# Post-norm transformer layer on eight cores: transposes moved from TensorE to the SP queue, and a different start

## The reference

```python
Q, K, V = x @ Wq + bq, x @ Wk + bk, x @ Wv + bv      # 16 heads of 64
w = softmax(causal(Q @ K.T / 8))                     # per sequence and head
x = layernorm(x + (w @ V) @ Wo + bo)                 # Wo 1024 x 1024
gate, up = x @ wg.T, x @ wu.T                        # int32 weights / 127, hidden 3072
x = layernorm(x + (silu(gate) * up) @ wd.T)
```

## Time and the profile before

| | |
|---|---|
| median of 3 runs | 1165.81 us (1165.63 to 1166.45) |
| profiled execution, device time | 1166.87 us |
| its span on the slowest core (2) | 1165.2 us |
| spans of the eight cores | 1160.5 to 1165.2 us |
| TensorE busy on core 2 | 1118.3 us, 96% of the span |
| ScalarE, VectorE, Pool busy | 602.1, 390.9 and 87.9 us |
| chain that ended last | PE 93%, issue 2%, DMA 2%, DVE 2%, ACT 1% |

### The profile page before, as it was taken

One profiled execution on the slowest core, in us unless ns is written; L12 is line 12 of the kernel. 1 busy time (PEld: TensorE's weight loads), 2 busy tenths in 40 slices (PEclk: granted clock), 3 DMA queues, 4 the chain that ended last, 5 costly groups with the idle time before them and its releaser, 6 DMA issues.

```text
span 1165.2 us, 28546 instructions; the slowest of 8 cores (1160.5 to 1165.2 us)
## 1 busy us (share of the span) xinstructions
PE 1118.3 (96%) x11460; PEld 676.3 (58%) x11568; DVE 390.9 (34%) x833; ACT 602.1 (52%) x723; POOL 87.9 (8%) x156
## 2 busy tenths in 40 slices
PE   3899999999999999999999999999999999999997
PEld 1676677767676677765555566666444444444443
DVE  0333323333333433335667522222333212121333
ACT  0588889999999899898855411112000111111000
POOL 3000000000000000013010211111000111110000
PEclk9999999999999999999999999999999999999999
DMA  9902100021001103069655764334111345441011
GB/s 128 155 3 38 21 2 3 2 39 21 2 3 21 20 3 74 33 153 244 138 129 109 147 107 73 63 65 73 37 55 55 74 75 82 78 73 19 37 45 66
DMA packets 32200, 74.61 MB, mean 64 GB/s; under 512 B 3648, under 2 KB 9792, under 8 KB 31168
## 3 DMA queue, kind: packets, MB, share of 16 engines
q0 software_dynamic: 26448, 54.80, 28.4%
q1 hardware_dynamic: 5616, 17.91, 4.1%
HBM read 109.65 MB, written 8.91 MB: 102 GB/s over the span
## 4 chain that ended last, share of the span: by engine, by line
PE 93%; issue 2%; DMA 2%; DVE 2%; ACT 1%; POOL 0%; POOLq 0%; DVEq 0%; ACTq 0%
PE ps_s L850 15%; PE ps_s L856 15%; PE bank_o L826 11%; PE ps_s L794 11%; PE ps_s L767 10%; PE ps_u L697 7%; PE ps_u L716 7%; PE ps_u L708 5%; PE ps_u L767 5%; PE ps_u L732 4%; DMA x<-x 2%; PE ps_s L732 1%; PE bank_o L746 1%; ACT PT L897 1%; PE ps_s L753 0%
## 5 line engine op out<-in xcount | busy, mean ns | idle before, releaser
L897 ACT ACTIVATE PT<-ps_s 128x1024 bf16<-128x1024 f32 x510 | 490.2, 1024 | 56.0 <-PE ps_s L794 48.9
L911 ACT ACTIVATE gs<-ps_s 128x384 bf16<-128x384 f32 (+1 forms) x120 | 63.9, 533 | 260.3 <-PE ps_s L850 260.1
L850 PE MATMUL ps_s<-x1T,wgb 128*128 128x384 bf16 (+1 forms) x953 | 195.5, 347 | 0.4
L856 PE MATMUL ps_s<-x1T,wub 128*128 128x384 bf16 (+1 forms) x952 | 195.3, 347 | 0.4
L826 PEld LDWEIGHTS bank_o<-V,PT 128*128 128x128 bf16 x4080 | 155.8, 97 | 46.9 <-issue 23.1
L826 PE MATMUL bank_o<-V,PT 128*128 128x65 bf16 x4080 | 176.4, 193 | 2.4 <-DVE PT L1006 2.0
L794 PE MATMUL ps_s<-Q2T,K2T 64*128 64x256 bf16 (+1 forms) x2736 | 158.4, 244 | 4.0 <-ACT PT L897 1.5
L1028 DVE TENSOR_TENSOR hT<-ps_s,gs 128x384 bf16<-128x384 f32 (+1 forms) x120 | 73.3, 611 | 264.3 <-PE ps_s L856 252.7
L850 PEld LDWEIGHTS ps_s<-x1T,wgb 128*128 128x128 bf16 x960 | 93.8, 98 | 83.2
L856 PEld LDWEIGHTS ps_s<-x1T,wub 128*128 128x128 bf16 x960 | 93.9, 98 | 82.6
L767 PE MATMUL ps_s<-wd_sb,hT 128*128 128x512 bf16 x541 | 120.2, 379 | 0.6
(11 more groups left out here) (57 smaller groups left out, 599.2 us busy)
## 6 DMA issues: line engine op xcount, KB each, us to landing
wgb<-wg POOLq DMA_DIRECT2D x48, 256.0 KB, 4.1
wub<-wu POOLq DMA_DIRECT2D x48, 256.0 KB, 5.1
xq_sb<-bo SPq DMA_DIRECT2D x17, 512.0 KB, 5.2
xq_sb<-xq POOLq DMA_DIRECT2D x17, 512.0 KB, 11.1
y<-y SPq DMA_DIRECT2D x17, 512.0 KB, 2.7
wd_sb<-wd POOLq DMA_DIRECT2D x6, 1024.0 KB, 14.2
x<-x POOLq DMA_DIRECT2D x4, 1024.0 KB, 28.2
wk_sb<-wk POOLq DMA_DIRECT2D x8, 256.0 KB, 4.6
```

The costliest lines, as they stand in the source:

```text
L850: inst = pe.matmul(ps_s[w % 2][:, 0, 0:n], wgb[:, i % 4, ec, :], x1T[:, ec, q:q + n], start=(ec == 0), stop=(ec == NEC - 1))
L856: inst = pe.matmul(ps_s[w % 2][:, 1, 0:n], wub[:, i % 4, ec, :], x1T[:, ec, q:q + n], start=(ec == 0), stop=(ec == NEC - 1))
L897: act.activation(PT[:, no % NSLOT], ps_s[no % 3][:], AF.Exp, scale=SCALE).then_inc(sem_exp, 1)
L911: act.activation(gs[:, no % 2, 0:n], ps_s[no % 2][:, 0, 0:n], AF.Silu, scale=1.0 / 127.0).then_inc(sem_silu, 1)
```

## The change

- The transposes of `o_nat` and of `x1` leave TensorE. SP issues a transposing transfer for each 128x128 block: one or two per block of attention (`rows_in`) and eight per set (`rows_on`), straight into `o_allT` and `x1T`. SP follows VectorE's list, so the loads of bo stand between them in that order. The units T, the transposes behind a block and VectorE's copies are gone.
- The waits move with them. The first wave of a part waits for all the sets of its part (`sem_xt`), a W unit for the transfers of its block (`sem_ot`), and a divide for those of the block two before.
- bv is added when V is copied out of PSUM (an addition in place of a copy), from a tile that holds bv for all 128 partitions (512 KB in place of 4 KB), loaded behind the constants. bo for sets 2 and 3 is loaded at the start.
- The W units may start six steps behind the end of their own block, before five behind the end of the next one.
- TensorE makes 16 products of zeros at the start, three between pieces of x block 0 and six ahead of the first V. Each has 512 columns.
- wk of pair 1 is asked for right behind wv. K(1,0) is done behind V of block 0 in both roles. In role 1 Q(0,0) and Q(0,1) follow it, and K(1,i) goes with block i.

```diff
+            return [('K', 0, 0), ('V', 0, 0), ('V', 0, 1), ('K', 1, 0), ('K', 0, 1), ('Q', 0, 0), ('V', 0, 2),
+                    ('V', 0, 3)]
...
             out += [('K', 0, i), ('V', 0, 2 * i), ('V', 0, 2 * i + 1)]
+            if i == 0:
+                out += [('K', 1, 0), ('Q', 0, 0), ('Q', 0, 1)]
+            else:
+                out += [('K', 1, i)]
             if i == 1:
-                out += [('Q', 0, 0), ('Q', 0, 1)]
...
-        block = self.block_end.index(h)
-        if block:
-            self.pe.append(('O', block - 1))
-        return block
+        return self.block_end.index(h)
...
-            first = self.block_end[nb * (NPAIR - 1) + qt // 2 + 1] // (4 * STEP) + 5
+            first = self.block_end[nb * (NPAIR - 1) + qt // 2] // (4 * STEP) + 6
             rows += [(first, self.steps, ('W', qt, 0)), (first, self.steps, ('W', qt, 1))]
-            if qt:
-                rows.append((first, self.steps, ('T', qt - 1)))
...
+            def rows_in(b):
+                sp.wait_ge(sem_o, b + 1)
+                p, q, n = block_rows(b)
+                for i in range(n // 128):
+                    sp.dma_start(o_allT[:, p, q + 128 * i:q + 128 * i + 128], o_nat[:, b % 2, i, :],
+                                 transpose=True).then_inc(sem_ot[b % 2], 16)
+            def rows_on(qt):
+                sp.wait_ge(sem_n, qt + 1)
+                g = next(i for i, sets in enumerate(plan.groups) if qt in sets)
+                for ec in range(NEC):
+                    sp.dma_start(x1T[:, ec, qt * 128:(qt + 1) * 128], x1[:, qt, ec * 128:(ec + 1) * 128],
+                                 transpose=True).then_inc(sem_xt[g], 16)
...
+            load_bo(2)
+            load_bo(3)
+            for what, no in plan.dve:
+                if what == 'D':
+                    rows_in(no)
+                elif what == 'N' and no < role.nset:
+                    rows_on(no)
...
+            def busy(n):
+                for _ in range(n):
+                    pe.matmul(ps_s[0][:, 0, :], PT[:, 0, 0, 0:128], PT[:, 0, 0, :], start=True, stop=True)
...
                         if a == 0 and i == 0 and ec % 2 == 0:
+                            if ec:
+                                busy(3)
                             pe.wait_ge(sem_x0[ec // 2], 16)
...
                     if first == 0 and unit in plan.first_of:
+                        if a == 0:
+                            busy(6)
                         pe.wait_ge(sem_wv[a % 2], 16 * (a // 2 + 1))
...
-                if hc == 0 and plan.done('T', (q + n - 1) // 128) > seen_ev:
-                    seen_ev = plan.done('T', (q + n - 1) // 128)
-                    pe.wait_ge(sem_ev, seen_ev)
+                if hc == 0:
+                    g = next(k for k, sets in enumerate(plan.groups) if (q + n - 1) // 128 in sets)
+                    pe.wait_ge(sem_xt[g], 16 * NEC * len(plan.groups[g]))
...
-                if b:
-                    rows_in(b - 1)
+                if b >= 2:
+                    dve.wait_ge(sem_ot[b % 2], ot_count(b - 2))
...
             for name, dst in consts:
                 sp.dma_start(dst[:], d[name]).then_inc(sem_const, 16)
+            sp.dma_start(bv_sb[:], d['bv']).then_inc(sem_bv, 16)
...
             pool.dma_start(wv_sb[:, 0], d['wv'][0]).then_inc(sem_wv[0], 16)
+            pool.dma_start(wk_sb[:, 1], d['wk'][1]).then_inc(sem_wk[1], 16)
             pool.dma_start(wq_sb[:, 0], d['wq'][0]).then_inc(sem_wq[0], 16)
...
+            pe.wait_ge(sem_zero, 1)
+            for _ in range(16):
+                pe.matmul(ps_s[0][:, 0, :], PT[:, 0, 0, 0:128], PT[:, 0, 0, :], start=True, stop=True)
```

More of the change, by code:

```diff
@@ L108, in __init__ @@
         self.tiles = [range(h, min(h + 4, n)) for h in range(0, n, 4)]
+        ends = sorted({t[-1] for t in self.tiles} | set(self.block_end))
+        self.pv_count = {h: i + 1 for i, h in enumerate(ends)}
         self.steps = -(-len(self.tiles) // STEP)
@@ L148, in __init__ @@
             self.pass_end.append(len(self.waves) - 1)
+            for q in parts:
+                have = sum(map(len, self.groups))
+                self.groups.append(range(have, -(-(q + part) // 128)))
             q0 = q1
@@ L367, in _network @@
     def _network(self):
-        role, nb = self.role, len(self.block_end)
+        role = self.role
         ring = itertools.cycle((0, 2, 1))
@@ L487, in build @@
     sem_pv = sem('sem_pv')
-    sem_block = sem('sem_block')
+    sem_bv = sem('sem_bv')
     sem_rec = sem('sem_rec')
     sem_o = sem('sem_o')
-    sem_tr = sem('sem_tr')
-    sem_ot = sem('sem_ot')
+    sem_ot = [sem(f'sem_ot{i}') for i in range(2)]
     sem_bn = sem('sem_bn')
@@ L497, in build @@
     sem_n = sem('sem_n')
+    sem_xt = [sem(f'sem_xt{i}') for i in range(5)]
     sem_g = sem('sem_g')
@@ L579, in block_rows, with ot_count, load_bo @@
             return b // nblock, *role.blocks[b % nblock][:2]
+        def ot_count(b):
+            return 16 * sum(block_rows(i)[2] // 128 for i in range(b % 2, b + 1, 2))
         def sync_program(sp):
-            for qt in range(role.nset):
-                if qt < 2:
-                    sp.wait_ge(sem_unit, plan.all_done('V', 3))
-                elif qt == 5:
-                    sp.wait_ge(sem_unit, plan.all_done('K', 7))
-                    sp.wait_ge(sem_unit, plan.all_done('Q', 7))
-                elif qt >= 12:
-                    sp.wait_ge(sem_ev, plan.done('W', xq_slot(qt), 1))
-                sp.dma_start(xq_sb[xq_slot(qt)][:], d['bo']).then_inc(sem_bo[xq_slot(qt)], 16)
+            def rows_in(b):
[10 more added lines that the diff above has]
+                                 transpose=True).then_inc(sem_xt[g], 16)
+            def load_bo(qt):
+                sp.dma_start(xq_sb[xq_slot(qt)][:], d['bo']).then_inc(sem_bo[xq_slot(qt)], 16)
+            load_bo(2)
[5 more added lines that the diff above has]
+                    rows_on(no)
+                elif what == 'E' and no + 1 == plan.all_done('V', 3):
+                    sp.wait_ge(sem_ev, no + 1)
+                    for qt in (0, 1, 4):
+                        load_bo(qt)
+                elif what == 'E' and no + 1 == max(plan.all_done('K', 7), plan.all_done('Q', 7)):
+                    sp.wait_ge(sem_ev, no + 1)
+                    for qt in range(5, 12):
+                        load_bo(qt)
+                elif what == 'E' and plan.units[no] in [('W', xq_slot(qt), 1) for qt in range(12, role.nset)]:
+                    sp.wait_ge(sem_ev, no + 1)
+                    load_bo(plan.units[no][1] + 8)
@@ L649, in gpsimd_program @@
                 load_qk(p)
-            pool.wait_ge(sem_pv, plan.block_end[nblock * 6 - 1] // 4 + 1)
+            pool.wait_ge(sem_pv, plan.pv_count[plan.block_end[nblock * 6 - 1]])
             pool.dma_start(wo_sb[:], d['wo']).then_inc(sem_wo, 16)
-            for qt in range(5):
+            for qt in (2, 3, 0, 1, 4):
                 add_rows(qt)
@@ L664, in load_wd @@
                 pool.dma_start(wd_sb[:, 4 * c:4 * c + 4], d['wd'][:, 4 * c:4 * c + 4]).then_inc(sem_wd, 16)
[L667 removed]
+            pool.wait_ge(sem_pv, len(plan.pv_count))
             for c in range(3):
                 load_wd(c)
[L671 removed]
             load_gu(4)
+            for i in range(2):
+                pool.wait_ge(sem_ot[i], ot_count(len(plan.block_end) - 1 - (len(plan.block_end) - 1 - i) % 2))
             for c in range(3, 6):
@@ L884, in tensor_program @@
                     products(no)
-                elif what == 'O':
-                    block_out(no)
                 else:
```

102 lines of the change are left out of this document (29 added, 73 removed).

## The result

The changed kernel takes 1222.02 us (median; 1220.8 to 1223.49) beside 1165.81 us: a ratio of 1.048 with an interval of 1.046 to 1.050, 56 us slower where 13 us faster was forecast, and outside the range.

What follows compares the result with a forecast made beforehand. TensorE was taken to bound nearly everything. On core 2, 1165.2 - 15.0 - 1.6 + 3.7 = 1152.3 us; the slowest span falls 12.9 us, so 1165.8 becomes 1153 us. The range of 8 in 10 was 1149 to 1172 us.

Steps and rivals of the forecast that it cites:

- What leaves TensorE: Attention-output and row-set transposes, 55 ns each: role 0 saves 15.0 us, role 1 13.2 us, plus 1.6 us on core 2.
- The start: Wait for x block 1: lands 5.4 us later; after work moved in, role 0 loses 3.7 us, role 1 1.9 us.
- Zero products and V's addition: Start and V's copy out of PSUM: neither gains; copy 694 ns, addition 692 ns, zeros' saved time spent waiting.
- the transfers on SP: Transposes on SP's queue at about 0.8 us each: hidden throughout attention and the last pair, so costing nothing.
- I take t at about 0.8 us: Queue time per transpose on SP, between the mask transfer's 0.43 us issue and 2.0 us landing.
- 71 t - 80.2: Wait in us of role 1's wave 4 for 71 transposes at t us each; none up to t = 1.13 us.
- 81 t - 101.1: Core 2's wave 8: 81 transposes at t us each against 101.1 us of room; hidden up to t = 1.25 us.
- the rival (0.30): SP's queue sets the output rows' pace: wave 4 of role 1 waits once t exceeds 1.13 us; chance 0.30.
- In attention a block needs two in 5 to 15 us: always: Attention: SP's transposes for a block are always hidden, at any t considered.
- leave more room or about as much: First waves, a block's divide and five late bo loads: no tighter for SP's transposes than the last pair's waves.
- the rival's 1178 us: SP's queue pacing the output rows: at t = 1.5 us, 26 us of wait at wave 4; rival's chance 0.30.
- By it the prediction had no change: With 1309 ns of queue time per transpose, role 1 waits 12.7 us; whole about 1165 us, no measurable change.

Runs made afterwards that it cites:

- late_held: Kernel before with wk_alone's start and second-pass row sets transposed by SP's transfers, held until wave 24's up products are done: 1161.65 us (0.996).
- wk_alone: Kernel before with only wk of pair 1 early and K(1,0), plus role 1's two Q units, in the wait for x: 1165.51 us (0.9995).
- mix_held: late_held plus attention output of pairs 0 to 6 by SP's transfers with four buffers, V's bias added at its copy from early 128 KB: 1162.58 us (0.9975).
- start_only: The change without any transposing transfer; its start's loads, K order, zero products and V's addition stay: 1170.56 us (1.004).
- loads_alone: Kernel before with only bv whole, two loads of bo ahead of x's block 1, and V's addition: 1170.68 us (1.004).
- late_sets: Kernel before with only the second-pass row sets transposed by SP's transfers, asked for as they are normalised: 1171.13 us (1.004).
- light: The change with wd's loads each one more gate/up tile later and only 128 of 1024 columns of xq and bo loaded: 1204.1 us (1.032).
- the two halves: The change with only attention output by transfers, 1186.64 us (1.017), and with only row sets by transfers, 1199.35 us (1.028).
- bo_pool: The whole change with bo asked for on Pool's queue in place of SP's: 1210.71 us (1.038).

## Why the prediction was wrong, point by point

*What leaves TensorE: right for the row sets, half right for the blocks.* Core 2 has 272 fewer products. The 64 transposes of row sets that late_held moves bring 3.9 us beside wk_alone, where 3.5 were counted. The block transposes bring less. Between the 101st and the 3001st product with V the change gains 5.3 to 5.6 us over the kernel before on the cores of role 0, but wk_alone, which moves K(1,0) and no transpose, gains 2.9 to 3.0. So the 95 block transposes between bring 2.4 to 2.6 us of the 5.2 counted, and mix_held has half of its count too. Why is open.

*The start: right in cause, a little short.* Block 1 was forecast at 33.2 us and came at 34.51 (34.55 on core 3, 34.1 forecast). The forecast of +3.7 us for role 0 stands beside 3.8 us of the whole in start_only and 4.5 in loads_alone (which has none of wk's load and of K(1,0), so 3.8 by the forecast's terms), and wk's load against K(1,0) comes to nothing, as counted.

*Zero products and V's addition: right.* V's copy took 694 ns, the addition takes 693. The zeros ended before what they precede, the clock behind the wait was 0.76 and 0.56 in two stretches of 2.5 us, as in the earlier trace rows, and nothing was gained.

*The step that failed: the transfers on SP.* Three sentences of it were wrong. The first is "I take t at about 0.8 us": an issue takes 1.20 us at the median of core 3 and never less than 1.08, and where it counted, over the 71 up to wave 4 of role 1, it is 1.57 us from one to the next, outside what hides it. The text's own 71 t - 80.2 gives 31 us at 1.57, and 26.3 us were measured. On core 2, the slowest, the 81 up to wave 8 come 1.52 us apart; 81 t - 101.1 gives 22 of the 28.1 us, and the last landing, 16.16 us where 2.0 were counted, is the rest by size. So the mechanism of the rival (0.30) was at work, and the size that was taken for t came from the wrong row. The mask's transfer shares size and shape, but it is 128 rows and no transpose.

The second is "In attention a block needs two in 5 to 15 us: always": it counted SP's time and not the landing. A landing of 2 to 3 us is hidden by two buffers. One of 14 to 28 us isn't, as core 2 has them beside the loads of wo and xq and then of bo, xq and the first gate and up tiles. The third says that the first waves and the divide "leave more room or about as much". The divide cost 19.8 us of TensorE on core 2 and 15.3 on core 3, and the first wave 9.7 us on core 3. Both were named and priced at nothing in every case. On core 3 they are 25 of the 35 us by which it passed even the rival's 1178 us.

*What was missing besides*: that a transpose delays the loads beside it (late_sets; the two waits for wub, 4.5 us together on core 2), and that a slow clock follows each stall. On core 2 that is 6.9 us up to the first wave, by the three stretches above, and 1.6 us behind the stall of 28 us.

*The pages.* The Trainium skill, "VectorE: DVE Perf Modes", The three transpose paths, has 1309 ns for one such transpose through the DMA engines; the trace's 1.2 us of the queue's own time is near it. By it the prediction had no change; the stretch beside the loads, the landings and the slow clock came on top. The Trainium skill, "Advanced Engine Details and Errata", X-Bar Transpose (TRN2), has transposes as fast as other transfers: the trace disagrees, 131 against 375 GB/s, and the measurement decides.

*Open*: the tail of 2 to 3 us in role 0, what stretches the issues in light, why the block transposes bring only half of what was counted, and the 7 us between the two halves (48.7 us with one start) and the whole (56); that both kinds stand in one queue would fit and was not separated.

## What to carry to other kernels

A transfer that replaces work of an engine has three prices: the time of its queue, its landing beside the largest loads that ever run with it, and what it adds to the landing of those. Read all three from a row of the same kind, or measure one such transfer, before the sum is made; the work taken off the bounding engine was small change here (55 ns each at most) beside a price of over 1 us of queue. Where such transfers can be held until the loads are through and their consumer is far off, they pay: that version, late_held, is the fastest measured, with mix_held within 1 us of it.

## What the runs showed of the hardware

In the change a transfer with transposition of 128x128 in bf16 makes about 159 packets under 512 bytes and takes 0.25 us of all 16 engines. The 120 of core 2 beside which that core loads nothing else hold SP's queue for 1.09 us at least, 1.2 us at the median and 2.5 us at most, and land after 2.2 us at least and 2.4 us at the median. With a burst of loads beside them they land after 12 to 28 us on this core, and an issue stretches to as much as 7.1 us, and to 7.7 us in bo_pool, where bo is on Pool's queue. In late_sets the loads beside such transposes land two to three times later (wub's 256 KB at 16.2 us in place of 5.9). Behind TensorE's stall of 28 us it ran at a clock of 0.50, the 1.2 GHz level, and it was at 1.00, the 2.4 GHz level, again from 700 us on; core 2:

```profile
690.00:695.00 5.00, 0.85 (x3) 0.43 (x4) 0.00 (x0) 0.00 (x0) 0.00 (x0) 0.50 0.94 135
695.00:700.00 5.00, 5.00 (x22) 2.44 (x21) 0.56 (x1) 2.96 (x3) 0.92 (x2) 0.75 0.14 30
700.00:705.00 5.00, 5.00 (x30) 2.73 (x28) 3.60 (x6) 2.16 (x5) 0.67 (x2) 1.00 0.88 148
```
